# A sandwich layer (windowed attention, ternary feed-forward) on one core: where the raw feed-forward weights are staged, in what order the start is loaded, and which engine does the norms, high halves and last norm

## The reference

```
x = x + layernorm(attn(layernorm(x), W_qkv, W_out, b_out))
x = x + layernorm(ffn(layernorm(x), W_up, W_gate, W_down))

attn: q, k, v from x @ W_qkv (16 heads of 32), rotary tables on q and k,
      scores masked to j <= i and j >= i - 128, softmax, @ v, @ W_out + b_out
ffn:  w -> clip(round(w / s), -1, 1) * s  with  s = mean(|w|) + 1e-8, for each of the three matrices
      hidden = silu(x @ up.T) * (x @ gate.T);  hidden @ down.T
```

## Time and profile before

| | us |
|---|---|
| median of 3 runs | 1393.1 (1392.79 to 1395.48) |
| the profiled execution's own time | 1396.07 |
| its span, first to last instruction | 1394.2 |
| PE busy | 1311.8 (94% of the span) |
| DVE busy | 899.7 (65%) |
| ACT busy | 785.2 (56%) |
| POOL busy | 694.9 (50%) |

### The profile page before, as it was taken

How to read it: one execution, slowest core, us unless ns; L and a number is a source line. 1 busy time by engine, 2 the same in 40 slices (tenths; PEclk the granted TensorE clock), 3 DMA queues, 4 the chain that set the end, 5 groups by cost and what they waited for, 6 DMA issues and landing times.

```text
span 1394.2 us, 28306 instructions
## 1 busy us (share of the span) xinstructions
PE 1311.8 (94%) x10094; PEld 928.5 (67%) x10094; DVE 899.7 (65%) x2367; ACT 785.2 (56%) x1521; POOL 694.9 (50%) x952
## 2 busy tenths in 40 slices
PE   6567798999999999999999999999999999999997
PEld 3355565776767767777767767776767776766774
DVE  5455687877667776776667776776767676634332
ACT  4477778655646565555646556565655545533332
POOL 2334566643646365553656355553657354425433
PEclk9788999999999999999999999999999999999999
DMA  8577765564675636675575736664474636411000
GB/s 301 154 226 208 230 170 160 128 146 93 138 161 112 139 82 148 137 156 90 132 157 123 148 82 140 138 152 100 120 146 103 152 80 139 88 38 31 24 14 26
DMA packets 346573, 178.18 MB, mean 128 GB/s; under 512 B 268096, under 2 KB 321728, under 8 KB 346432
## 3 DMA queue, kind: packets, MB, share of 16 engines
q1 hardware_dynamic: 344704, 170.06, 53.1%
q10 hardware_dynamic: 1728, 6.29, 1.4%
HBM read 84.48 MB, written 25.17 MB: 79 GB/s over the span
## 4 chain that ended last, share of the span: by engine, by line
PE 84%; ACT 3%; DMA 3%; DVE 3%; issue 3%; POOL 2%; SPq 1%; POOLq 0%; DVEq 0%; ACTq 0%
PE J L1268 27%; PE Y L1283 15%; PE J L1211 14%; PE J L1202 7%; PE J L1219 7%; PE S L1268 4%; PE O L1187 4%; PE S L1155 3%; PE J L1233 1%; DMA W<-in_w_qkv 1%; ACT prob L756 1%; DMA spill<-split 1%; PE Y L1163 1%; ACT turned L765 1%; POOL room L663 0%
## 5 line engine op out<-in xcount | busy, mean ns | idle before, releaser
L1283 PE MATMUL Y<-down_q,room 128*128 128x512 fp8e4 x1024 | 262.2, 379 | 1.0 <-POOL room L648 1.0
L1211 PE MATMUL J<-xnT,W 128*128 128x512 f32 x512 | 242.1, 602 | 4.6 <-ACT xnT L740 3.2
L756 ACT ACTIVATE prob<-prob,peak 128x256 f32<-128x256 f32 x512 | 229.8, 498 | 25.5 <-DVE peak L990 25.3
L990 DVE CUSTOM_DVE_ANT_0 prob<-S,band,neg_score_scale 128x256 f32<-128x256 f32 x512 | 225.8, 478 | 26.0 <-PE S L1152 20.7
L1268 PE MATMUL J<-xT,gate_q 128*128 128x256 f16 x1760 | 211.8, 274 | 4.8 <-DVE room L1044 4.8
L1268 PE MATMUL J<-xT,up_q 128*128 128x256 f16 x1776 | 212.0, 273 | 0.7 <-DVE room L1052 0.7
L1268 PEld LDWEIGHTS J<-xT,gate_q 128*128 128x128 fp8e4 x1760 | 172.0, 98 | 50.8 <-DVE room L1044 10.2
L636 POOL TENSOR_TENSOR o_n<-o_raw,rinv 128x128 f32<-128x128 f32 x128 | 54.3, 424 | 302.8 <-DVE rinv L1019 302.8
L1268 PEld LDWEIGHTS J<-xT,up_q 128*128 128x128 fp8e4 x1776 | 173.4, 98 | 44.6 <-DVE room L1052 2.1
L807 ACT ACTIVATE room<-J,sig_scale 128x512 f32<-128x512 f32 x111 | 76.0, 685 | 222.8 <-PE J L1268 222.7
L1044 DVE SCALAR_TENSOR_TENSOR room<-room,J 128x512 f32<-128x512 f32 x111 | 76.1, 686 | 170.4 <-ACT room L807 170.2
(11 more groups left out here) (119 smaller groups left out, 1997.6 us busy)
## 6 DMA issues: line engine op xcount, KB each, us to landing
spill<-split SPq DMA_DIRECT2D x64, 256.0 KB, 2.7
Qp<-spill SPq DMA_DIRECT2D x128, 128.0 KB, 2.9
Kp<-spill SPq DMA_DIRECT2D x128, 128.0 KB, 3.0
x_in<-in_x SPq DMA_DIRECT2D x32, 256.0 KB, 3.5
room<-in_w_down SPq DMA_DIRECT2D x16, 512.0 KB, 3.9
X<-in_x SPq DMA_DIRECT2D x32, 256.0 KB, 3.3
out_x<-X SPq DMA_DIRECT2D x32, 256.0 KB, 2.9
room<-in_w_gate SPq DMA_DIRECT2D x12, 512.0 KB, 5.8
```

Of the source, the lines that this page charges most:

```text
L756: e = nc.scalar.activation(prob[:, U % PROBS, a, :], prob[:, U % PROBS, a, :], ACT.Exp, bias=peak[:, U % PROBS, a:a + 1], scale=-1.0)
L990: e = nc.vector.tensor_tensor_reduce(out=prob[:, U % PROBS, a, :], in0=S_ps[U % 2][:, a * 2 * P:(a + 1) * 2 * P], in1=mask[:], scale=neg_s ...
L1211: e = pe.matmul(dst[:], W[:, part, c, g * P:(g + 1) * P], xnT[:, c, :], start=(c == 0), stop=(c == DC - 1))
L1283: e = pe.matmul(Y_ps[t][:], h[:, q % HELD, part, (a * HT + t) * P:(a * HT + t + 1) * P], down_q[:, 2 * pair + a, :], start=(pair == 0 and ...
```

## The change

1. **Staging.** The sums use all four pieces of `room` throughout. The rounding gets three pieces of its own, which lie where nothing else is yet needed: `parts`, `y2` and the second half of `xT`. SP may load piece m once piece m-3 is signed (before: m-2). The matrix of ones moves from `y2` to `xf`, which makes the first write of `xf` wait for the last of the three totals.
2. **Timing of both readings.** Only 8 chunks are summed ahead of the loop (before 16); the other 40 go into slots 2 to 33, five in four slots. Rounding starts in slot 9 instead of 6, its loads three slots before it instead of two; POOL rounds first in its slot instead of last. The three means are made in slots 8, 21 and 36 (before 2, 19, 34).
3. **The start.** W_qkv is loaded through ACT's queue, its third part in two halves with a maximum each; ACT's first sum loads wait for the last of it. On SP both spills of a group are issued ahead of its two packs, and the second tile of x is loaded after the first packs.
4. **POOL for ACT.** Up to slot 55 POOL does the high half of Q and K, the norm of x and the norm of y.
5. **The end.** DVE does the last low half, takes the last two statistics from PSUM directly, and does the shift arithmetic but for the power; ACT normalises from PSUM; DVE adds the residual.

```diff
-AHEAD = 12
-SUMMED = 16
-CUT_FIRST = 6
+AHEAD = 4
+SUM_FIRST = 2
+CUT_FIRST = 9
+EARLY = 56
-SUM_SLOTS = {2: 0, 19: 1, 34: 2}
+SUM_SLOTS = {8: 0, 21: 1, 36: 2}
-        raw = room[:].rearrange("p (b n) -> p b n", b=4)
+        sum_raw = room[:].rearrange("p (b n) -> p b n", b=4)
-        ones = y2[:, 0, 0:P]
+        ones = xf[:, 0:P]
+        cut_raw = [parts[:].bitcast(F32).rearrange("p b s k -> p (b s k)"), y2[:].rearrange("p t d -> p (t d)"),
+                   xT[:, 1].bitcast(F32).rearrange("p t c q -> p (t c q)")]
...
+        def sum_slot(c):
+            return SUM_FIRST + (c - 2 * AHEAD) * 4 // 5
...
-            engine.dma_start(where, weights(n, k * PIECE)).then_inc(sum_loaded[sum_home(m)], 16)
+            engine.dma_start(where, weights(n, k * PIECE)).then_inc(sum_loaded[m % 4], 16)
...
-                at_least(sp, cut_done, 2 * (m - 1))
-                if m < 2:
-                    sp.wait_ge(abs_done, 2 * AHEAD)
-                where = raw[:, 2 + m % 2, :]
+                at_least(sp, cut_done, 2 * (m - 2))
+                where = cut_raw[m % 3]
...
-            for part in range(3):
-                sp.dma_start(W[:, part], w_qkv[part].rearrange("(c p) n -> p c n", p=P)).then_inc(w_in[part], 16)
...
+            spill_q(0, 0)
+            spill_k(0, 0)
+            pack_q(0, 0)
+            pack_k(0, 0)
+            for m in range(AHEAD, 3 * PIECES):
+                if sum_slot(2 * m) - 4 < 0:
+                    load_for_sum(sp, m)
             for t in range(TT):
                 load_x(1, t)
-            spill_q(0, 0)
-            pack_q(0, 0)
-            spill_k(0, 0)
-            pack_k(0, 0)
...
-                    if s == max(2 * m - SUMMED - 4, 0):
+                    if s == sum_slot(2 * m) - 4:
                         load_for_sum(sp, m)
-                    if s == CUT_FIRST + 2 * m - 2:
+                    if s == CUT_FIRST + 2 * m - 3:
                         load_for_cut(m)
...
+            def high(i, a, g):
+                pool.tensor_scalar(split[:, a, 0], rot[:, a, :], 1.0, None, ALU.mult).then_inc(r_hi_done, 1)
+            def layer_norm(i, t):
+                pool.tensor_scalar(x_in[:, t, :], x_in[:, t, :], rstd_x[:, t:t + 1], shift_x[:, t:t + 1],
+                                   ALU.mult, ALU.add).then_inc(xn_done, 1)
+            def y_normalise(n):
+                pool.tensor_scalar(y_sb[:, n % 2, :], y_sb[:, n % 2, :], rstd_y[:, t:t + 1], shift_y[:, t:t + 1],
+                                   ALU.mult, ALU.add).then_inc(yn_done, 1)
...
             for s in range(END):
                 i, u = divmod(s, UNITS)
+                for c in cut_chunk_at(s):
+                    to_whole(c)
...
+                src = y2[:, t, :]
+                if n >= (HALVES - 1) * HT:
+                    src = Y_ps[t][:]
...
+            for part in range(2):
+                act.dma_start(W[:, part], w_qkv[part].rearrange("(c p) n -> p c n", p=P)).then_inc(w_in[part], 16)
+            for c in range(0, DC, 2):
+                act.dma_start(W[:, 2, c:c + 2], w_qkv[2, c * P:(c + 2) * P].rearrange("(c p) n -> p c n", p=P)
+                              ).then_inc(wv_in[c // 2], 16)
...
+            act.wait_ge(wv_in[1], 16)
+            for m in range(AHEAD):
+                load_for_sum(act, m)
+            for c in range(4):
+                absolute_sum(c)
...
+            hidden_low(ALL_PAIRS - 1)
+            for t in range(HT):
+                last_statistics((HALVES - 1) * HT + t)
+            for t in range(HT):
+                last_shift((HALVES - 1) * HT + t)
+            for t in range(HT):
+                finish((HALVES - 1) * HT + t)
```

More of the change, by code:

```diff
@@ L376, in weights, with cut_chunk @@
             return rows[:, first:first + PIECE // cols, :]
-        def sum_home(m):
-            return m % 4 if m < AHEAD else m % 2
-        def sum_turn(m):
-            return sum(sum_home(k) == sum_home(m) for k in range(m + 1))
         def load_for_sum(engine, m):
             n, k = divmod(m, PIECES)
-            earlier = [j for j in range(m) if sum_home(j) == sum_home(m)]
-            if earlier:
-                engine.wait_ge(abs_done, 2 * (earlier[-1] + 1))
-            where = raw[:, sum_home(m), :]
+            at_least(engine, abs_done, 2 * (m - 3))
+            where = sum_raw[:, m % 4, :]
             if n == 2:
                 where = where.rearrange("p (c n) -> p c n", n=D)
-            engine.dma_start(where, weights(n, k * PIECE)).then_inc(sum_loaded[sum_home(m)], 16)
+            engine.dma_start(where, weights(n, k * PIECE)).then_inc(sum_loaded[m % 4], 16)
+        def cut_chunk(c):
+            return cut_raw[c // 2 % 3][:, c % 2 * CHUNK:(c % 2 + 1) * CHUNK]
         block = ctx.enter_context(nc.Block())
@@ L689, in _ @@
                     rstd_of_x(i + 1)
+                if 11 <= u < 11 + TT and s < EARLY:
+                    layer_norm(i + 1, u - 11)
+                for kind, t, tile in ENDS[s - 3] if 3 <= s else ():
+                    if kind == "Y" and s - 3 < EARLY:
+                        y_normalise(tile * TT + t)
                 for kind, t, tile in ENDS[s - 1] if s >= 1 else ():
@@ L706, in _ @@
                         if s == first + 2 * (PAIRS + DOWN_LAG) - 2 + t + 2:
[L707 to L708 removed]
+                            if half == HALVES - 1:
+                                power_of_z(half * HT + t)
+                            else:
+                                rstd_of_z(half * HT + t)
+                        if s == first + 2 * (PAIRS + DOWN_LAG) - 2 + t + 4 and half < HALVES - 1:
                             finish(half * HT + t)
@@ L907, in _ @@
                             z_normalise(half * HT + t)
-                        if s == first + 2 * (PAIRS + DOWN_LAG) - 2 + t:
+                        if s == first + 2 * (PAIRS + DOWN_LAG) - 2 + t and half < HALVES - 1:
                             z_copy(half * HT + t)
@@ L1124, in _ @@
                             ff_low(half * HT + t)
-                        if s == first + 2 * (PAIRS + DOWN_LAG) - 2 + t + 1:
+                        if s == first + 2 * (PAIRS + DOWN_LAG) - 2 + t + 1 and half < HALVES - 1:
                             z_statistics(half * HT + t)
```

126 lines of the change are left out of this document (79 added, 47 removed).

## The result

| | us |
|---|---|
| before, median of 4 runs | 1392.94 (1391.90 to 1395.48) |
| changed, median of 4 runs | 1384.87 (1383.00 to 1385.30) |
| ratio | 0.9937, 95% interval 0.9920 to 0.9954 |
| profiled execution: own time, span | 1385.30, 1383.5 |

The change takes 8.1 us off, not 35. The forecast of 1358 is wrong, and its range, 1342 to 1374, doesn't hold the time.

What follows compares the result with a forecast made beforehand. PE is never short of work from slot 58, so gains lie in the first 254 us and last 15: -10.6 - 5.6 - 9.1 - 7.0 - 2.8 = -35.1 from 1396.07, less 2.97 against the median: 1358 us, range 1342 to 1374.

Steps and rivals of the forecast that it cites:

- What bounds the kernel, and the sign: All to win lies in the first 254 us and the last 15, PE being never short from slot 58; faster 0.96.
- Slots 0 to 9, -5.6: Slots 0 to 9: two waits of 5.43 and 3.19 us go, 3.0 us lost to a new one; range -3 to -10.
- the term of piece 6: Slots 0 to 9: SP loads piece 6 for the sums late, ACT wants it in slot 5; 3.0 us lost.
- Start, -10.6: Up to the first score: W_qkv complete at 15.7, first score at 39.5 instead of 50.1; range -9.6 to -12.9.
- Slots 10 to 33, -9.1: Slots 10 to 33: third buffer and earlier load remove most waits, 85.9 to 76.8 us; range 0 to -15.7.
- the transfers become the bound: Rival: transfers keep slots 10 to 33 at 85.9 us, other stages gain less; -19.1, 1374 us, chance 0.16.
- Slots 34 to 57, -7.0: Slots 34 to 57: two thirds of the time above PE's busy 69.3 us goes, leaving 71.4; range -4 to -9.1.
- The work on POOL: Norms and high halves moved to POOL: 17.5 us, up to 32, hidden behind PE and ACT.
- End, -2.8: After ACT's last copy: 7.7 us becomes about 5.4, and the last low half gets faster on DVE; range -2.3 to -3.1.

Runs made afterwards that it cites:

- e1: The changed kernel with the bias load issued ahead of group 1's spills instead of behind their packs; 1372.83 us, ratio 0.9858.
- e14: The changed kernel with only the bias load moved right behind the masks, ahead of all spills; 1374.05 us, ratio 0.9873.
- e12: e8 with ACT's p_high ahead of its copies of V and oT in the slot instead of behind; 1364.95 us, ratio 0.9806.
- e13: e12 with the bias loaded right behind the masks, ahead of the first spill; 1365.45 us, ratio 0.9812.
- e3: e1 with two staging pieces for the rounding instead of three, loaded two slots ahead instead of three; 1384.48 us, ratio 0.9937.
- e4: e1 with W_qkv back on SP's queue behind x and the identity, ahead of tables and masks; 1368.90 us, ratio 0.9830.
- e11: e8 with POOL's rounding last in its slot, as before the change, instead of first; 1374.30 us, ratio 0.9883.
- e15: e12 with 16 chunks summed ahead of the loop instead of 8, pieces 4 to 7 loaded by ACT at the start; 1367.04 us, ratio 0.9817.
- e5: e4 with the loop's raw-weight loads cut to 256 of 1024 columns, output not the reference's; 1364.84 us, ratio 0.9803.
- e7: e4 with both small loads and small sums, the cuts of e5 and e6 together; 1361.80 us, ratio 0.9781.
- e6: e4 with each sum inside the loop reading 32 of 512 columns, output not the reference's; 1367.84 us, ratio 0.9824.
- e2: e1 with norms of x and y and the high halves back on ACT (EARLY = 0); 1370.63 us, ratio 0.9837.
- e8: e4 with POOL taking norms and high halves only up to slot 33 instead of 55; 1366.31 us, ratio 0.9818.

## Why the prediction was wrong

*What bounds the kernel, and the sign:* right. What could be won lay ahead of slot 58 and at the end, and slots 58 on moved by 0.9 us.

*Slots 0 to 9, -5.6:* the step that failed. I listed the orders of SP for the term of piece 6, wrote that the bias and W_out now stand behind the packs of group 1, and asked only who waits for piece 6. Who waits for the bias, DVE ahead of slot 0, I did not ask. A load that was covered before became the end of a chain: 12.0 us (e1), 10.8 by e14. Without it the stage gives -7.9 (e1), and the term was good. The wait for piece 6, 3.0 us in the sum, lay hidden behind the longer one in the changed kernel; with the bias earlier it shows, in the slot that I named, with 1.1 us in e1, 1.0 in e14, 2.0 in e12 and 4.3 in e13.

*Start, -10.6:* direction right, size 6.8 us at the first score, a third term that was mis-sized. The bytes came as I summed them: 359 GB/s to 10 us, 388 to 15 us, nothing more from 16 to 19 us; I had W complete at 15.7. What failed is x. I gave it half of the rate and 8.0 us; its last block came at 10.46, by when some 3.1 MB had moved (an estimate from 294 GB/s over 10.46 us), of which x is 1.05. So PE started at 14.48, not at 12.0. V's matmuls ended at 32.0, not at 27.0: the other 2.4 us are the step that took 9.54 us instead of 7.10, for which the sum had nothing, and which e3, with this start, did in 7.1 (its first score comes at 40.2). So of the 3.8 us missed here, some 2.4 may be chance of this execution. K's low half came at 35.1 instead of 30.1, and from there the score took 8.1 us instead of 9.4. The maximum at 18.1 (17.6 forecast) was not what held it: DVE had scaled the tables by 21.4 and began on Q at 25.1. The Trainium skill (DMA: Bandwidth & Descriptors, "Issuing engines are not separate DMA queues") says that transfers from different issuing engines interleave on the same engines; the trace agrees: with W on ACT's queue the rate is no higher (359 to 388 GB/s against 364 to 402 before), and x comes later. I had given that 1.6 us of the start; e4 gets 3.9 back at the median.

*Slots 10 to 33, -9.1:* the second step that failed; the stretch gave -0.6. I said that the waits for the rounding would go, and they went (33.1 to 10.1 us in all). Of their causes I had named the two pieces (e3) and not POOL's order, which alone brings 23.5 us of them back (e11). What was wrong is that the length would follow. Two things took their place. The eight sums that no longer lie ahead of the loop: 3.4 us in this stretch (e15). The transfers, of which those sums' loads are a part: 5.5 us (e5). My rival "the transfers become the bound" named the length rightly, 85.9 us, but by luck: the transfers make up only that part of it, and the share was 0.77, not near 1. (Its sum takes 2.5 us for the end, where the range of that term stops at 2.3.) ACT's place in line, behind PE's banks, may be another part, but e12 doesn't show it. The two overlap, and 3.25 us per slot without loads and sums (e7) remain where PE is busy for 2.74; what sets that pitch I leave open. I had set ACT's 70.2 us beside the length and called the difference a margin; ACT was busy 70.65, and e6 took 12 us of its work away and got 0.8.

*Slots 34 to 57, -7.0:* got -3.3. The work on POOL, which I let hide behind PE and ACT, did not hide: with it back on ACT this stage takes 72.7 to 73.2 us at the same clock of 1.00, not 75.1 (e2, e8). The high half is a mis-sized term in it: I took 0.70 us, with 1.3 as the upper bound, and it takes 1.50. That it is the high halves and not the norms is not shown, as they moved together. Some 1.3 to 1.8 us of the miss, from 71.4 up to these 72.7 to 73.2, stay unexplained.

*End, -2.8:* -3.2 measured. Statistics from PSUM took 0.70 us, those from SBUF 0.69. The Trainium skill (VectorE: DVE Perf Modes, "The TRN2 errata — SBUF-src ops pay a fixed extra latency per instruction") would have PSUM 0.06 us longer; these rows do not show it.

*Sum of the misses,* by windows: 3.8 for the start, 9.8 for slots 0 to 9, 8.5 for slots 10 to 33, 3.7 for slots 34 to 57, less 1.3 for what lies behind them: 24.5, as the spans have it within rounding (-10.7 instead of -35.1). The rest of the 26.9 between forecast and median is the 2.97 that I took off because the profiled execution before lay so far above its median; that of the changed kernel lies 0.43 above.

## What to carry to other kernels

When instructions are moved on an in-order DMA queue, list what every load that now stands behind a waiting one is waited for by, down to the smallest: here a bias of 512 numbers cost as much (12.0 us, e1) as the third piece for the rounding gained (11.7, e3). A wait that goes is worth only the distance to the next one behind it (in e13 the bias's wait went, and the one for piece 6 stood there); leave out the work of each engine in turn before you call one the bound, and compare two windows only after you know how far equal code differs. And if an operation writes another type than the rows you price it by, give its price a wide bound.

## What was not expected of the hardware

- POOL's tensor_scalar takes 0.70 us from f32 to f32 (128x512, x16 per buffer) and 1.50 us from f32 to f16 (x13), though its two-input subtraction with the same f16 output takes 1.16.
- x (1 MB) and W_qkv (3 MB), issued side by side by SP and ACT: the last block of x landed at 10.46 us, when some 3.1 MB had moved. Behind each other on SP's queue, x was there over 4 us earlier (e4).
- The bias, issued right behind two sum loads and four of x, landed 7.85 us after its issue in e12; in the changed kernel, issued at 56.54, after 5.07.
- In the changed kernel PE's weight loads for L1290 start 0.85 us apart from 19.9 to 23.3 us and 0.43 from 24.0 on, at a granted clock of 1.00 throughout; the sixteen matmuls took 9.54 us. In ten of the seventeen profiled executions, the one before the change among them, this step took 7.1, in the other seven 8.8 to 9.6, whatever the kernel, and the granted clock was 1.00 in all of them.
- PE's granted clock in slots 34 to 57 was 1.00 in some runs and 0.98 in others: for e12 and e13, with the same code there, 0.98 at 74.6 us and 1.00 at 72.9, PE busy 1.7 us longer in the former. It does not explain all lengths: 78.4 (before), 77.4 (e3) and 75.1 us (the changed kernel) came at 1.00 too.
